# Self-attention with keys and queries in two one-pass 32-bit pieces, heads in pairs on the two halves of the array

## The reference, cut to what matters

```python
q = (x @ wq).reshape(B, T, H, D)
lat = x @ w_down
k = (lat @ wk_up).reshape(B, T, H, D)
v = (lat @ wv_up).reshape(B, T, H, D)
q = _apply_rope(q, cos, sin)
k = _apply_rope(k, cos, sin)
scores = jnp.einsum('bqhd,bkhd->bhqk', q, k) * scale
pages = jnp.arange(T) // PAGE_SIZE
allowed = pages[None, :] <= pages[:, None]
scores = jnp.where(allowed[None, None], scores, jnp.finfo(scores.dtype).min)
attn = jax.nn.softmax(scores, axis=-1)
out = jnp.einsum('bhqk,bkhd->bqhd', attn, v).reshape(B, T, E)
return out @ wo
```

## Time and profile before

| | us |
|---|---|
| median of three runs | 823.3 (823.13 to 825.24) |
| the profiled execution's own time | 824.24 |
| its span, first to last instruction | 822.5 |
| attention loop within the span | 92.7 to 531.0 |

### The profile page before, as it was taken

How to read it: one execution, slowest core, us unless ns; L and a number is a source line. 1 busy time by engine, 2 the same in 40 slices (tenths; PEclk the granted TensorE clock), 3 DMA queues, 4 the chain that set the end, 5 groups by cost and what they waited for, 6 DMA issues and landing times. The chain is left out here.

```text
span 822.5 us, 12183 instructions
## 1 busy us (share of the span) xinstructions
PE 755.3 (92%) x4329; PEld 393.8 (48%) x4329; DVE 620.3 (75%) x1107; ACT 427.4 (52%) x879; POOL 149.9 (18%) x170
## 2 busy tenths in 40 slices
PE   8874887999999999999999998899868999999997
PEld 5431232333223333222333231287547888888886
DVE  4899687888998899999898760067614778778786
ACT  1552463676667776657777867822123333333353
POOL 2564000000000000000000000013141455555520
PEclk9986797999999999999999998999999999999999
DMA  7796321120000000000440000030001222222103
GB/s 209 207 266 202 87 76 39 33 59 27 1 2 2 1 2 2 1 2 0 158 142 1 2 0 2 3 110 1 0 1 41 80 81 80 80 80 80 40 1 103
DMA packets 27152, 47.32 MB, mean 58 GB/s; under 512 B 6112, under 2 KB 23008, under 8 KB 26336
## 3 DMA queue, kind: packets, MB, share of 16 engines
q1 hardware_dynamic: 25184, 43.94, 17.8%
q10 hardware_dynamic: 1920, 2.75, 1.2%
HBM read 38.16 MB, written 8.39 MB: 57 GB/s over the span
## 5 line engine op out<-in xcount | busy, mean ns | idle before, releaser
L486 DVE TENSOR_REDUCE part_max<-psum 128x1 f32<-128x512 f32 (+3 forms) x560 | 341.4, 669 | 55.0 <-PE psum L672 50.0
L591 ACT ACTIVATE probs<-psum 128x512 f32<-128x512 f32 (+3 forms) x640 | 293.7, 539 | 155.5 <-PE psum L697 154.5
L672 PE MATMUL psum<-k_stack,q_stack 96*128 96x512 bf16 (+4 forms) x640 | 214.9, 364 | 18.6 <-DVE psum L472 11.2
L697 PE MATMUL psum<-q_stack,k_stack 98*128 98x512 bf16 (+4 forms) x640 | 202.3, 357 | 13.1 <-DMA q_stack<-shift 11.3
L709 PE MATMUL psum<-probs,v_all 128*17 128x512 f32 (+3 forms) x1280 | 149.7, 540 | 0.3
L672 PEld LDWEIGHTS psum<-k_stack,q_stack 96*128 96x128 bf16 (+1 forms) x640 | 60.1, 99 | 171.9 <-DVE part_max L486 121.5
L697 PEld LDWEIGHTS psum<-q_stack,k_stack 98*128 98x128 bf16 (+1 forms) x640 | 60.9, 99 | 94.3 <-ACT probs L591 39.2
L1471 PE MATMUL psum<-ctx_part,qc_part 128*128 128x512 f32 (+1 forms) x384 | 84.7, 371 | 5.0 <-POOL qc_part L1253 4.1
L877 POOL MEMSET eps<- 128x4 f32 x1 | 0.1, 102 | 459.6 <-POOLq L273 459.6
L1545 PE MATMUL psum<-v_parts,p_part 128*128 128x512 f32 (+3 forms) x416 | 76.9, 341 | 0.0
L1471 PEld LDWEIGHTS psum<-ctx_part,qc_part 128*128 128x128 f32 x384 | 67.3, 192 | 18.9 <-issue 4.9
(11 more groups left out here) (140 smaller groups left out, 681.6 us busy)
## 6 DMA issues: line engine op xcount, KB each, us to landing
mask<-in_mask SPq DMA_DIRECT2D x16, 800.5 KB, 4.4
pieces<-k_stack SPq DMA_DIRECT2D x24, 256.0 KB, 5.0
q_stack<-pieces SPq DMA_DIRECT2D x24, 256.0 KB, 4.2
k_stack<-pieces SPq DMA_DIRECT2D x24, 256.0 KB, 4.7
x_sb<-in_x SPq DMA_DIRECT2D x4, 512.0 KB, 8.9
out<-x_sb SPq DMA_DIRECT2D x8, 256.0 KB, 2.2
q_stack<-in_ctxT SPq DMA_DIRECT2D x1, 1601.0 KB, 11.1
probs<-in_cos ACTq DMA_DIRECT2D x4, 256.0 KB
```

Of the source, the lines that this page charges most:

```text
L486: nc.vector.tensor_reduce(part_max[:, h:h + m, r, c:c + 1], src, axis=AX_X, op=ALU.max).then_inc(m_read, 1)
L591: nc.scalar.activation(probs[:, s % 2, h, col:BLK], s_bank[h][:, col:BLK], ACT.Exp, scale=ATTN_SCALE).then_inc(exp_done, 1)
L672: last = nc.tensor.matmul(out, q_stack[b][0:rows, g * G + h, r * P:(r + 1) * P], k_stack[c][0:rows, g * G + h, 0:keys], start=True, stop=True)
L697: nc.tensor.matmul(s_bank[h][:, col:BLK], k_stack[s // TPB][0:rows, g * G + h, (s % TPB) * P:(s % TPB + 1) * P], q_stack[b][0:rows, g * G ...
```

## The change

Queries and keys are cut into two pieces of the one-pass 32-bit type (float32r) and three products are kept, so that a head needs 48 + 2 + 4 = 54 rows. Even and odd heads of a group share a tile: one in partitions 0 to 53, the other in 64 to 117 (`PAR`, `ROOM`), with matmuls issued in pairs. A maxima unit is now two heads of up to 512 keys in two neighbouring banks, reduced by one VectorE instruction; there are two such pairs of banks (`m_pair`), and the score banks are three (`S_BANKS`), taken in turn. The plan's numbers are halved (`AHEAD`), `TURN_LAG` is 2.

The second piece is the remainder itself, so the second `cut` and `last_piece` go, on ScalarE, VectorE and GpSimd. The pieces to HBM are 16 transfers of 512 KB in place of 24 of 256 KB. All loads of the stacks, the constant rows and the shifts are issued by GpSimd: constant rows of blocks 0 and 1 ahead of the first `rotate`, the 12 loads of block 0 ahead of the third `rotate`, those of block 1 ahead of the fourth, and those of block 2 and of block 3 in one piece each, after the shift of the second and of the fifth group. The maxima are cut into two pieces ahead of the turn, by two VectorE operations; one copy follows it. TensorE waits for a block's stacks at the third group of the block before, and runs 32 more warm-up matmuls behind the front's last product.

```diff
-Q_PIECES = [0, 0, 0, 1, 1, 2]
-K_PIECES = [0, 1, 2, 0, 1, 0]
+Q_PIECES = [0, 0, 1]
+K_PIECES = [0, 1, 0]
+PIECES = 2
 COPIES = len(Q_PIECES)
+PAR = 2
+HP = H // PAR
+ROOM = P // PAR
...
-TURN_LAG = 3
-
-AHEAD = [(10, 10), (14, 14), (18, 18), (24, 24)]
+TURN_LAG = 2
+
+AHEAD = [(5, 5), (7, 7), (9, 9), (12, 12)]
...
-    s_bank = [banks(psum, h) for h in range(G)]
-    o_bank = banks(psum, 4)
-    m_bank = [banks(psum, n) for n in (5, 6, 7)]
+    S_BANKS = 3
+    s_bank = [banks(psum, n) for n in range(S_BANKS)]
+    o_bank = banks(psum, 3)
+    m_pair = [banks(psum, n, PAR) for n in (4, 6)]
...
             norm(0)
             norm(1)
             norm(2)
+            for b in range(2):
+                load_extra_rows(nc.gpsimd, io, q_stack[b], k_stack[b], extra_loaded[b])
             for tb in range(NB):
                 rotate(tb)
-                last_piece(tb)
                 if tb == 0:
                     norm(3)
+                if tb:
+                    for n in range(PIECES):
+                        if tb < NB - 1:
+                            load(tb - 1, n)
+
+            def load_late(b):
+                load_extra_rows(nc.gpsimd, io, q_stack[b], k_stack[b], extra_loaded[b])
+                for n in range(PIECES):
+                    load(b, n)
+
+            send_shift(0, 0)
+            pool.wait_ge(prod_done, 8 * NB)
+            pool.wait_ge(v_ready, 2 * NB)
+            for n in range(PIECES):
+                for r in range(2):
+                    pool.wait_ge(piece_sent[n][r], 16 * NB)
+            for k, (b, g) in enumerate(order):
+                if k:
+                    send_shift(b, g)
+                if k in (1, NG):
+
+                    pool.wait_ge(shift_sent, 16 * PAR * (k + 1))
+                    load_late(2 + k // NG)
...
+                        heads, r, c, keys = units[b][n]
+                        for m, at_h in enumerate(heads):
+                            h = g * (G // PAR) + at_h
+                            for par in range(PAR):
+                                out = pair[:, par * BLK + m * keys:par * BLK + (m + 1) * keys]
+                                rows = slice(par * ROOM, par * ROOM + (STACK if c == b else TERM_ROWS))
+                                last = nc.tensor.matmul(out, q_stack[b][rows, h, r * P:(r + 1) * P],
+                                                        k_stack[c][rows, h, 0:keys], start=True, stop=True)
                         last.then_inc(m_ready, 1)
...
-            def scores(b, g, s, h):
+            def scores(b, g, s, half):
                 n = s_base(b, g) + s
                 col = first_col(b, s)
-                if n:
-
-                    pe.wait_ge(exp_done, (n - 1) * G + h + 1)
-                rows = STACK if s >= TPB * b else SHIFTED
-                nc.tensor.matmul(s_bank[h][:, col:BLK],
-                                 k_stack[s // TPB][0:rows, g * G + h, (s % TPB) * P:(s % TPB + 1) * P],
-                                 q_stack[b][0:rows, g * G + h, col:BLK], start=True, stop=True).then_inc(s_ready, 1)
+                heads = range(half * PAR, half * PAR + PAR)
+                taken = n * G + heads[-1] + 1 - S_BANKS
+                if taken > 0:
+
+                    pe.wait_ge(exp_done, taken)
+                for h in heads:
+                    rows = slice(h % PAR * ROOM, h % PAR * ROOM + (STACK if s >= TPB * b else SHIFTED))
+                    at = g * (G // PAR) + h // PAR
+                    nc.tensor.matmul(s_bank[(n * G + h) % S_BANKS][:, col:BLK],
+                                     k_stack[s // TPB][rows, at, (s % TPB) * P:(s % TPB + 1) * P],
+                                     q_stack[b][rows, at, col:BLK], start=True, stop=True).then_inc(s_ready, 1)
...
+            pe.wait_ge(xt_copied, NB * EC)
+            for n in range(32):
+                nc.tensor.matmul(x_bank[n % 2], warm[:, 0:P], warm[:, P:P + BLK], start=True, stop=True)
             pe.wait_ge(o_cleared, 1)
```

More of the change, by code:

```diff
@@ L237, in self_attention @@
     starts = [sum(len(p) for p in parts[:n]) for n in range(len(parts))]
-    part_banks = [[1 if n == len(p) - 1 and n % 3 == 0 else n % 3 for n in range(len(p))] for p in parts]
-    bank_of = sum(part_banks, [])
-    def since(n, at):
-        at += starts[n]
-        return next((d for d in range(1, at + 1) if bank_of[at - d] == bank_of[at]), None)
     def entries_of(b, g):
         k = b * NG + g
-        for at, (what, kk, n) in enumerate(parts[k + 1]):
-            yield what, *order[kk], n, starts[k + 1] + at, since(k + 1, at), m_bank[part_banks[k + 1][at]]
+        for at, (what, kk, n) in enumerate(parts[k + 1], starts[k + 1]):
+            yield what, *order[kk], n, at, m_pair[at % 2]
     def s_base(b, g):
@@ L469, in _ @@
                     norm(tb + 2)
-            last_piece(NB - 1)
             nc.vector.memset(o_bank, 0.0).then_inc(o_cleared, 1)
             def maxima(entries):
-                for what, b, g, n, at, _, bank in entries:
+                for what, b, g, n, at, pair in entries:
+                    bank = pair[:, 0:BLK]
                     dve.wait_ge(m_ready, at + 1)
@@ L725, in group @@
                         done = due
-                        pe.wait_ge(shift_sent, (index(*where) + 1) * 16 * SHIFT_ROWS)
-                    for h in range(G):
-                        scores(*where, s, h)
-                        due = len(entries) * (sum(weights[:i]) + weights[i] * (h + 1) / (G + 1)) // sum(weights)
+                        pe.wait_ge(shift_sent, (index(*where) + 1) * 16 * PAR)
+                    for half in range(G // PAR):
+                        scores(*where, s, half)
+                        due = len(entries) * (sum(weights[:i]) + weights[i] * (half + 1) / (G // PAR)) // sum(weights)
                         maxima(entries[done:int(due)])
@@ L1597, in build @@
                 keep["v_parts"] = same_place.enter_context(nc.sbuf_tensor("v_parts", [P, S2_TILES, 2, E], F32R))
-            first_stacks = [sbo(f"q_stack{b}", [P, H, BLK], BF16) for b in range(NB - 1)]
+            with ExitStack() as same_place:
+                keep["q_room"] = [same_place.enter_context(nc.sbuf_tensor(f"q_room{b}", [P, HP, BLK], F32))
+                                  for b in range(NB - 1)]
+            first_stacks = [sbo(f"q_stack{b}", [P, HP, BLK], F32R) for b in range(NB - 1)]
             with ExitStack() as early:
```

249 lines of the change are left out of this document (106 added, 143 removed).

## The result

The changed kernel takes 939.3 us in the median of four runs (928.4 to 949.4), the kernel before 823.9 beside it: 1.136 times as long (95% interval 1.125 to 1.146). The forecast was 853 with a range up to 880, so the sign was right and the size far off; the time lies nearest to the rival that had a chance of 0.03, the falling clock (926 us).

What follows compares the result with a forecast made beforehand. The prediction took TensorE's issue order as the bound, VectorE 12% behind. To the profiled 824.2 us it added terms stated as +31 together (front, blocks, last group), less 2 for partly hidden weight loads: 853 us, range 812 to 880.

Steps and rivals of the forecast that it cites:

- the falling clock: Rival: TensorE idle 0.6 us every step, clock swings to 1.2 GHz for half the loop; +73, 926 us; chance 0.03.
- second and third block at +0: Attention loop's second and third block: chain and VectorE group times together 225.9 us, as before, so 0 added.
- Pairs side by side: Score and maxima matmuls: two heads run at once in the array's halves, 0.22 us a pair at full clock.
- The chain through the step: Full loop step: second score pair waits for the first exponential, through P·V to next scores; period 2.82 us.
- The shift behind the loads: First block: third shift queues behind 16 GpSimd transfers, so TensorE waits 7 us (2 to 12).
- GpSimd's issues: Transfers on GpSimd's queue, front and loop: 0.84 us per issue, ends 0.3 and 1.1.
- a sign of being wrong: Listed observation that would show the forecast wrong, for GpSimd's queue: issues under 0.5 us.
- Lower clock in the first block, +2: First block, after TensorE's wait for the shift: some us run at 1.2 GHz, adding 2 us.
- the 2 us taken off: Deduction from the whole sum because weight loads may partly hide: less 2 us.

Runs made afterwards that it cites:

- the last group with its clock held: Changed kernel with three pairs of half-array filler matmuls on constants per step of the last group only: 922.6 us, 1.119 times the kernel before.
- the run with repeats: Changed kernel with the maxima matmuls between a step's two score pairs issued twice, plus half-array fillers in the last group: 910.9 us, 1.105.
- the run with four banks: Changed kernel with four score banks, single maxima banks, spread late loads and full-height fillers ahead of maxima matmuls in the first slot: 1144.1 us.

## Why the prediction was wrong, point by point

The step that failed is the granted clock: the sum priced all but a few microseconds of the loop at 2.4 GHz and gave a falling clock a chance of 0.03. The runs showed about 250 of the loop's 549 us at 1.2 GHz. A second term, second and third block at +0, was too small even at full clock.

- *Pairs side by side:* right. A score pair lasts 0.50 us at full clock and 0.79 at the low one.
- *The chain through the step:* right in shape and size for the last block. 2.89 us against 2.82; group 13, at full clock throughout, 44.2 us against 43.5; the last group with its clock held 38.1 against 38.6.
- *Second and third block, 0:* mis-sized. At full or nearly full clock (the run with repeats, at most 7.4 us low each) groups 4, 5, 6, 8, 9 and 10 take 24.3, 22.8, 26.3, 34.2, 33.0 and 39.6 us, 180.2 together; the forecast had 162.8. They hold 12.9 us of low clock and the repeats' own issue; groups 5, 6, 9 and 10 alone, with 2.2 us low, take 121.6 against 109.8. I had charged the chain to full steps and taken the rest for scaling with width. In group 5 of that run, at full clock throughout, the first four steps take 11.9 us and the last four, which narrow, 10.9 where 4 x 1.10 + 2.5 x 1.72 is 8.7: its excess lies in the narrow steps. The 16-bit kernel with three banks also loses there: 27.3 us more than before in these two blocks.
- *The shift behind the loads:* right. 8.47 us of waiting against 7. But undoing it gained nothing.
- *GpSimd's issues:* 0.48 us a load (four in 1.93) and 0.56 a shift, against 0.84 assumed. That is inside the bounds kept, but the loads are under the 0.5 that I had named as a sign of being wrong. The first maxima start at 72.9 us, not 77.7; before it was 74.8.
- *Lower clock in the first block, +2:* the step that failed first. TensorE waits 7.85 us ahead of the first maxima, and the clock falls in both kernels there; the 16-bit one has it back at 93.3 us (and loses it again from 134.3 to 147.9), the changed one at 184.2. The block takes 81.3 us against a forecast of 64.8.
- *The clock rival, 0.03:* the step that decided. Its argument against was one stretch, 104.1 to 107.5 us, in which TensorE was busy 2.19 of 3.40 and the clock stayed full. That row shows matmuls over the array's whole height; I read it as a statement on idle time and carried it to matmuls of another form. The price was too low as well: at 1.2 GHz P·V costs 0.85 us more, not 0.41, and a step of the last group 1.5 more, not 1.1. That the rival's 926 us lie so near is partly luck: its half of the loop was right, its price too low, and the mis-sized second and third block filled the gap.

By stretches, after against the forecast: first block +16.5, second and third +42.3, groups 12 and 13 +4.3, group 14 +1.0, last group +18.8, the start of the loop −6.0, behind it +3.4; with the 2 us taken off that makes 82.3 of the 84 between 853 and the profiled execution's 937.1 (1.1 more lie outside the span, and the sum's terms add to 31.5 where I wrote 31). Of the +42.3 roughly 11 us are not the clock's, by the four groups above; the last group's 18.8 are the clock's, by its fillers. For the first block no run held the new form at full clock throughout, so its share stays open.

The sentence on the Trainium skill ("TensorE: Matmul & The Clock Gate", A second HAM failure mode), that the trace speaks against swings of the clock under brief idle time, was right for the 16-bit form and wrong for the form that the change brings: there the clock fell nine times between 184.2 and 447.0 us.

## What to carry to other kernels

A change that halves the time that matmuls spend on the array, by packing two into its halves, can also take away what keeps the clock at 2.4 GHz, and here repeats and fillers gave back at most 29 of the 115 us lost; ask of every such saving what TensorE does in the freed time. A row that shows a full clock beside idle time holds only for the form of matmul in that row: rows of the array, type and pairing belong to the evidence. And a bank taken away from a pipeline that waits per step should be priced alone, on the old kernel, before it is mixed with anything else: here that one experiment (1.078) would have shown a loss twice as large as the one I forecast for the whole change.

## What the runs showed of the hardware

- The same 16-bit matmuls over 48 to 54 rows instead of 96 to 102, with TensorE busy all the time, run at a granted clock of 0.50 through whole groups (12 and 13: 78.49 of 78.49 us busy, 78.08 of 78.08); over all their rows, and idle a sixth to a third of the time, they keep 0.97 to 1.00 (43.83 of 53.07 us busy, 31.03 of 44.42).
- At the low clock eight P·V matmuls of 128x512 take 1.83 us to the next start against 0.98, a score pair lasts 0.79 against 0.50.
- Two matmuls in the two halves of the array finish in 0.50 us together at full clock; full-height matmuls between such pairs cost 0.09 us for the change of shape ahead of them (0.43 against 0.34) and about 0.2 behind them: two take 0.67 us to the next pair, where 23 of the warm-ups took 5.37 us in the changed kernel, 0.23 each.
- An issue from GpSimd takes 0.48 us for a load of 256 KB (four in 1.93) and 0.56 for a shift (median of 32).
- Full-height fillers among half-array pairs do not ensure the full clock: 58.18 us at 0.50, TensorE busy 57.99, in the run with four banks.
